# Splitting weights and building rotation tables in the first stage, keeping them in DRAM, and loading them per layer

## What is computed

```
for i in range(6):
    x = attn_layer(shift_tokens(x), Wqkv[i], q_scale[i], k_scale[i], Wo[i]) + x
    x = ffn_layer(shift_tokens(x), ln_g[i], ln_b[i], W1[i], b1[i], W2[i], b2[i]) + x

attn_layer:  q, k, v = split(x @ Wqkv)             # 128 -> 3 x 1024, 16 heads of 64
             q, k = l2norm(q) * q_scale, l2norm(k) * k_scale
             q, k = rotary(q), rotary(k)            # by position, with a scale
             out = local_attention(q, k, v) @ Wo    # windows of 32, each looks at itself and the one before
ffn_layer:   hg = (layernorm(x) * ln_g + ln_b) @ W1 + b1   # 128 -> 2 x 341
             a, gate = split(hg);  out = (a * gelu(gate)) @ W2 + b2
```

## Time and profile before

| | |
|---|---|
| runs of the kernel before | 3352.69, 3348.1, 3351.99 us; median 3351.99 |
| profiled execution | 3352.12 us, its span 3350.4 us |
| PE busy | 3196.8 us (95%) |
| POOL busy | 2967.1 us (89%) |
| DVE busy | 2747.9 us (82%) |
| ACT busy | 2740.7 us (82%) |
| TensorE clock over the span | 0.984 of full |
| DMA queue of the transfers | 226.85 MB, 25.3% of 16 engines |
| first stage / second stage | up to about 409 us / the rest |

### The profile page before, as it was taken

The page is one execution under the profiler, slowest core; times in us unless marked ns, Lnnn a source line. Parts: engine busy times, 40 slices in busy tenths (PEclk is TensorE's granted clock), DMA queues, the critical chain, the costliest instruction groups (busy, mean ns, idle before and its releaser), DMA issues.

```text
span 3350.4 us, 158044 instructions
## 1 busy us (share of the span) xinstructions
PE 3196.8 (95%) x64569; PEld 2754.7 (82%) x64570; DVE 2747.9 (82%) x5172; ACT 2740.7 (82%) x4528; POOL 2967.1 (89%) x3534
## 2 busy tenths in 40 slices
PE   7999669999999999999999999999999999999997
PEld 5676458888888888888888888888888888888886
DVE  7777577888888888888888888888888888888886
ACT  4677557888888888888888888888888888888885
POOL 5677578999999999999999999999999999989995
PEclk9999889999999999999999999999999999999998
DMA  2000013222223222223222233222232222332222
GB/s 62 5 8 8 16 39 90 76 75 72 66 72 99 75 74 68 67 75 102 75 70 68 70 96 81 70 68 75 69 102 74 68 72 63 82 91 73 75 66 74
DMA packets 162047, 228.51 MB, mean 68 GB/s; under 512 B 42392, under 2 KB 60768, under 8 KB 161760
## 3 DMA queue, kind: packets, MB, share of 16 engines
q1 hardware_dynamic: 161888, 226.85, 25.3%
HBM read 21.00 MB, written 4.19 MB: 8 GB/s over the span
## 4 chain that ended last, share of the span: by engine, by line
PE 65%; POOL 12%; issue 7%; ACT 2%; DVE 2%; POOLq 0%; SPq 0%; DMA 0%; DVEq 0%; ACTq 0%
PE ring L1418 9%; PE ring L1377 8%; PE ring L1427 8%; PE proj L1368 7%; PE score L1396 6%; PE proj L1370 6%; PE proj L1369 6%; POOL by_cos L1253 4%; PE ring L1403 4%; PE ring L1480 3%; PE ring L1471 2%; POOL weightsb L1264 2%; POOL by_cos L1259 2%; PE ring L1473 2%; PE ring L1472 2%
## 5 line engine op out<-in xcount | busy, mean ns | idle before, releaser
L1253 POOL TENSOR_TENSOR by_cos<-by_cos,by_sin 128x1024 f32<-128x1024 f32 x384 | 916.1, 2386 | 19.5 <-DVE by_sin L1654 19.4
L1259 POOL TENSOR_TENSOR by_cos<-by_cos,norms 128x1024 f32<-128x1024 f32 x384 | 731.6, 1905 | 20.1
L1652 DVE TENSOR_TENSOR by_cos<-proj,turns 128x512 f32<-128x512 f32 x768 | 521.7, 679 | 189.0 <-PE ring L1377 117.3
L1368 PE MATMUL proj<-qkv_hi,xs_hib 128*128 128x512 f32 x1152 | 535.5, 465 | 36.1 <-ACT vb L1515 16.0
L1654 DVE TENSOR_TENSOR by_sin<-proj,turns 128x512 f32<-128x512 f32 x768 | 522.5, 680 | 0.0
L1536 ACT ACTIVATE squares<-proj 128x512 f32<-128x512 f32 x768 | 444.1, 592 | 26.7 <-PE proj L1370 13.8
L1658 DVE TENSOR_REDUCE sumsb<-squares 128x16 f32<-128x1024 f32 x384 | 464.0, 1208 | 0.0
L1370 PE MATMUL proj<-qkv_hi,xs_lob 128*128 128x512 f32 x1152 | 459.5, 399 | 0.0
L1369 PE MATMUL proj<-qkv_lo,xs_hib 128*128 128x512 f32 x1152 | 459.2, 399 | 0.2 <-issue 0.2
L1377 PE MATMUL ring<-ident,by_cos 128*128 128x128 f32 x3072 | 413.2, 278 | 1.2 <-issue 1.2
L1418 PEld LDWEIGHTS ring<-pTb,v_win 64*64 64x64 f32 x24576 | 382.7, 136 | 36.7 <-issue 26.6
(11 more groups left out here) (188 smaller groups left out, 7349.7 us busy)
## 6 DMA issues: line engine op xcount, KB each, us to landing
v_win<-vb SPq DMA_DIRECT2D x1152, 128.0 KB, 2.3
v_win<-vb SPq DMA_DIRECT2D x768, 64.0 KB, 2.0
in_qkv<-L_ffn_Wqkv SPq DMA_DIRECT2D x12, 768.0 KB
wo<-L_ffn_Wo SPq DMA_DIRECT2D x12, 256.0 KB, 3.8
x_tok<-L_attn_x SPq DMA_DIRECT2D x8, 256.0 KB, 4.4
residual<-x_tok SPq DMA_DIRECT2D x8, 256.0 KB, 2.0
in_w<-L_ffn_W SPq DMA_DIRECT2D x12, 170.5 KB
in_qkv<-residual SPq DMA_DIRECT2D x1, 1536.0 KB, 6.7
```

The costliest lines, as they stand in the source:

```text
L1253: nc.gpsimd.tensor_tensor(both, both, by_sin[:, j, :], ALU.add).then_inc(e[f"{w_}_added"].sem, 1)
L1259: nc.gpsimd.tensor_tensor(heads, heads, inverse, ALU.mult).then_inc(e[f"{w_}_ready"].sem, 1)
L1368: nc.tensor.matmul(out, xs_hi[:, tile], qkv_hi[:, cols], start=True, stop=False)
L1652: nc.vector.tensor_tensor(of_heads(by_cos[:, t % 2, j, cols]), heads, table(0), ALU.mult)
```

## The change

- 48 pieces (36 of `Wqkv`, 128x512, and 12 of `W1`, 128x341) are split in the first stage. SP loads each four steps ahead, ScalarE copies the high part at the end of steps 1, 5, 7, 9, 13, 15 of each batch, VectorE subtracts one step later, SP stores the low part to DRAM. The `Wqkv` pieces of layer 0 come last and stay in SBUF.
- In batches 0 to 5 GpSimd makes the four tables of one layer at steps 5, 6, 12, 13, after `causal` and before `negated_maxima`. They are stored to DRAM, except those of layer 0, which stay.
- Per layer SP loads `Wqkv` and `W1` as before, and now their low parts too. ScalarE copies the high and then the low part of each `Wqkv` piece at the places of the `hi_*` pieces, and `NF` copies `w1_hi` and `w1_lo`. VectorE's `lo_*` and GpSimd's `turn_*` and `NL` are gone.
- The tables arrive by DMA (`Tq`, `Tk`), and `b1`, `ln_g`, `ln_b`, `W2`, `b2` (`FC`, `F2`, eleven transfers) go by DMA straight into the tiles in use.
- The second stage's prologue has no copies, subtracts or tables. The clears of `kT` and `v` are cut to the parts that are read before they are written, and the other padding is cleared by GpSimd there and no longer by VectorE at the start.

```diff
+SPLIT_AT = [MQA_H * b + h for b in range(B) for h in (1, 5, 7, 9, 13, 15)]
+TURN_AT = (5, 6, 12, 13)
...
             for n, b, h in steps():
                 if 0 <= n < HEADS:
                     causal(n)
+                if batch_of(b) and b < DEPTH and h in TURN_AT:
+                    rotation_table(DEPTH - 1 - b, TURN_AT.index(h))
                 if h % PER_GROUP == 1 and 0 <= (n + AHEAD) // PER_GROUP < B * GROUPS:
                     negated_maxima((n + AHEAD) // PER_GROUP)
...
+            def split_high(i):
+                kind, layer, k, slot, turn, cols = piece_of(i)
+                act.wait_ge(split_moved[slot], 32 * turn + 16)
+                copy(ready["hi"][:, cols], ready["in"][:, cols]).then_inc(split_hi, 1)
...
                     if 0 <= n < HEADS:
                         exps(n, k)
+                if n in SPLIT_AT:
+                    split_high(SPLIT_AT.index(n))
...
+            def split_low(i):
+                cols = piece_of(i)[-1]
+                dve.wait_ge(split_hi, i + 1)
+                nc.vector.tensor_tensor(ready["lo"][:, cols], ready["in"][:, cols], ready["hi"][:, cols].bitcast(F32),
+                                        ALU.subtract).then_inc(split_lo, 1)
...
+                if n - 1 in SPLIT_AT:
+                    split_low(SPLIT_AT.index(n - 1))
...
 NEXT_WEIGHTS = {
     "Act": {(-2, "aQq:3"): "hi_q0", (-2, "MK:1"): "hi_k0", (-2, "bQk:3"): "hi_k1", (-2, "GEL"): "hi_q1",
           (-1, "EV:1"): "hi_v0", (-1, "EK:0"): "hi_v1"},
-    "DVE": {(-2, "XM"): "lo_q0", (-2, "AM"): "lo_q1", (-2, "WX:-1"): "lo_k1", (-2, "XN"): "lo_v0 lo_k0",
-          (-1, "aCk:2"): "lo_v1"},
-    "Pool": {(-2, "Aq:3"): "turn_0", (-1, "Mk:0"): "turn_1", (-1, "Mq:1"): "turn_2", (-1, "Mk:1"): "turn_3"},
+    "SP": {(-2, "VM:1"): "Tq", (-1, "VM:0"): "Tk", (2, "VM:0"): "FC F2"},
 }
...
-            nc.gpsimd.memset(kT[:, :, :], 0.0)
+            nc.gpsimd.memset(kT[:, :, HS - WINDOW:HS], 0.0)
             nc.gpsimd.memset(sums[:, :, :, :, 1], L2_EPS2)
-            for n in range(TILES):
-                nc.gpsimd.memset(v[:, n, :, :, :], 1.0)
+            nc.gpsimd.memset(w2[:, FC - 1, :], 0.0)
+            for x in (in_w1, in_w1_lo):
+                nc.gpsimd.memset(x[:, :, FF:FC * P], 0.0)
+            nc.gpsimd.memset(col[:, :], 0.0)
...
                 elif kind[:3] == "hi_":
                     x = kind[3:]
-                    act.wait_ge(loaded, all_loaded(new))
-                    if when[1] >= 0:
-                        event, tile = f"{x[0]}_proj", PER * STEPS - 1 - PER * p
-                        wait_tile(act, event, tile, when, 1 + int(x[1]))
+                    act.wait_ge(qkv_loaded, new * 64)
+                    wait_tile(act, f"{x[0]}_proj", PER * STEPS - 1 - PER * p, when, 1 + int(x[1]))
                     cols = columns_of(x)
-                    copy(qkv_hi[:, cols], in_qkv[:, cols]).then_inc(p_hi[x], 1)
+                    copy(qkv_hi[:, cols], in_qkv[:, cols]).then_inc(p_qkv[x], 1)
+                    copy(qkv_lo[:, cols], in_lo[:, cols]).then_inc(p_qkv[x], 1)
                 elif kind == "NF":
-                    act.wait_ge(loaded, all_loaded(new))
-                    wait_half(act, "gated", when, 0)
-                    wait_half(act, "xn_lo", when, 0)
-                    copy(col[:, :], in_col[:, :]).then_inc(p_col, 1)
+                    act.wait_ge(w1_loaded, new * 48 + 48)
                     wait_half(act, "up_full", when, 0)
                     copy(w1_hi[:, :, :], in_w1[:, :, :]).then_inc(p_w1_hi, 1)
-                    wait_half(act, "y_full", when, 0)
-                    copy(w2[:, :, :], in_w2[:, :, :]).then_inc(p_w2, 1)
+                    copy(w1_lo[:, :, :], in_w1_lo[:, :, :]).then_inc(p_w1_lo, 1)
```

More of the change, by code:

```diff
@@ L118, in fills, with piece_of, mqa_stage @@
     return (3, FILLS * m), (2, FILLS * m + 1), (1, FILLS * m + 2)
-def mqa_stage(nc, c, semaphore, weights, x_in, credits, arrived, residual, first_layer):
+def piece_of(i):
+    kind, layer, k = SPLITS[i]
+    slot, turn = i % len(PIECES), i // len(PIECES)
+    n = INNER // 2 if kind == "qkv" else FF
+    return kind, layer, k, slot, turn, slice(slot * (INNER // 2), slot * (INNER // 2) + n)
+def mqa_stage(nc, c, semaphore, weights, x_in, credits, ready, kept, of_layer, tables_in, residual):
     with ExitStack() as ctx:
@@ new lines, in load_split, with store_split @@
+            def load_split(i):
+                kind, layer, k, slot, turn, cols = piece_of(i)
+                at_least(sp, split_moved[slot], 32 * turn)
+                if kind == "qkv":
+                    in_ = of_layer["Wqkv"][layer, :, k * (INNER // 2):(k + 1) * (INNER // 2)]
+                else:
+                    in_ = of_layer["W1"][layer, :, k * FF:(k + 1) * FF]
+                sp.dma_start(ready["in"][:, cols], in_).then_inc(split_moved[slot], 16)
+            def store_split(i):
+                kind, layer, k, slot, turn, cols = piece_of(i)
+                sp.wait_ge(split_lo, i + 1)
+                if kind == "qkv":
+                    out = kept["qkv"][layer, :, k * (INNER // 2):(k + 1) * (INNER // 2)]
+                else:
+                    out = kept["w1"][layer, :, k, :]
+                sp.dma_start(out, ready["lo"][:, cols].bitcast(F32)).then_inc(split_moved[slot], 16)
@@ L899, in steps_of @@
     if at == -LEAD:
-        steps += [((piece,), None, "", 0) for piece in " ".join(NEXT_WEIGHTS.get(engine, {}).values()).split()]
+        steps += [((piece,), None, "", 0) for piece in ("FC", "F2") if engine == "SP"]
     if at == -LEAD and engine == "SP":
@@ L911, in steps_of @@
             steps.append((("NO",), 0, "", tile // (PER * STEPS)))
-        if engine == "Pool" and name == "FP" and at is not None and at % STEPS == LAG and end is None:
-            steps.append((("NL",), 0, "", at // STEPS))
         steps.append(((name,), t, token, 0 if tile is None else tile // (PER * STEPS)))
@@ L1196, in new_layer @@
                 sp.sem_inc(sp_ready, 1)
-                load_layer(sp, arrived, w, layer + 1)
+                for k in range(2):
+                    half = slice(k * QKV // 2, (k + 1) * QKV // 2)
+                    sp.dma_start(in_qkv[:, half], w["Wqkv"][one, :, half].rearrange("a k n -> (a k) n")).then_inc(qkv_loaded, 16)
+                    sp.dma_start(in_lo[:, half], kept["qkv"][one, :, half].rearrange("a k n -> (a k) n")).then_inc(qkv_loaded, 16)
+                sp.wait_ge(p_w1_hi, layer + 1)
```

238 lines of the change are left out of this document (136 added, 102 removed).

## The result

The changed kernel takes 3330.28 us (median of 5; 3329.26 to 3337.39) against 3351.99 (median of 5): a ratio of 0.9944, with a 95% interval of 0.9930 to 0.9958. It is 0.56% faster. The prediction was 3344 with a range of 3326 to 3364: the sign and the range held, but the gain was 22 us in place of the forecast 8, nearly three times as much.

A forecast was written before the change was run, and what follows sets the result against it. TensorE was taken to bound the second stage, so only layer changes, prologue and first stage could move. -6.6 (prologue) - 18.6 (A) - 0.5 (B) + 17 (stage one) = -8.7 on 3352.1 gave 3344 us, range 3326 to 3364.

The forecast's parts named there:

- part A: Cycles renewing Wqkv pieces and tables at a layer change: excess 4.1 in place of 7.8 us, -18.6 us over five.
- The rule on the shared interface: VectorE with two SBUF inputs and GpSimd reading SBUF take turns, the later blocking for the whole other; speaks against the change.
- rival 4: Stage one: each of 48 subtracts costs its full 0.67 us beside GpSimd; 3363 us, 3373 with mutual waits; chance 0.14.
- Part B: Later cycle renewing FFN weights: `vb` wait some 0.2 us longer, `w_lo` gone; about -0.1 x 5, -0.5 us.
- Prologue: Start of stage two: narrow clears, no copies or subtracts, first projection earlier by 6.6 us (bounds -5.5 and -8).
- Stage one: First stage, which receives the 48 pieces and the tables: +17 us (bounds +5 to +37).
- The sum for the tables: Stage one, GpSimd tables: +0.6 us at h=5, +0.4 at h=13, others in idle time; 4.7 us over six batches.
- rival 1: Stage one hides the subtracts in VectorE's idle time; only about 5 us reach TensorE, 3332 us; chance 0.19.
- transitions nearly free: Layer changes: ScalarE's copies also find cover, A falls to about 1 us; 3329, with rival 1 3320; chance 0.08.
- Rival 3: Layer changes: ScalarE takes it back, doubled copies return the idle elsewhere, A gains at most 1 us each; 3357; chance 0.13.

The follow-up runs named there:

- the subtracts alone: Changed kernel with the six low parts of a layer change made again by VectorE's subtracts, without ScalarE's low copies; tables still by transfer: 3341.7 us.
- the products alone: Changed kernel plus four unused GpSimd products of 128x256 at a layer change, where the rotation tables were made before: 3344.4 us.
- both: Changed kernel with VectorE's subtracts back in place of ScalarE's low copies, and four GpSimd products at the old tables' places: 3350.7 us.

## Why the prediction was right, point by point

- **The layer change, part A.** An excess of 4.1 us in place of 7.8 was worked out, 3.8 measured: -19.9 us over five changes for -18.6. The steps behind it hold one by one: the mean 4.1 us late was worked out and 3.7 measured, the transpose of `weights` behind TensorE's own order, `weights` ready 1.0 us before it, the clock at 1.00. What the prediction left undivided, two causes of GpSimd's delay, the runs divide: the subtracts alone bring back 2.27 of the 2.90 us and the lower clock at two changes of five, the products alone nothing, both 2.72 us and the lower clock at all five.
- **The rule on the shared interface.** Each kernel with subtracts beside GpSimd in stage two shows an operation of 0.25 us that takes 2.6 and ends with the subtracts. In stage one a key spreading of 1.56 us takes up to 2.1 with a subtract beside it. The Trainium skill, SBUF — State Buffer, section "Who interferes with whom", says that a VectorE instruction with two inputs in SBUF contends with a GpSimd one that reads SBUF. The traces agree with that, but not with a block for the length of one other instruction, as the prediction put it: the GpSimd operation began before the subtracts and was held over three of them. The price in stage one was 0.2 us per subtract and not the 0.67 of rival 4.
- **Part B.** -0.1 us was forecast for each layer, -0.6 measured (1.9 to 1.3 over the cycles of that place). The wait for `vb` is as worked out (1.33 against 1.3). What failed is the reading of `w_lo`: the 0.27 us that I took for the lateness of `f_rstd` is only GpSimd's idle time between the two instructions. In the kernel before:

```profile
1005.50 0.16 DVE L1727 TENSOR_SCALAR f_varb<-ring 128x2 f32<-128x2 f32 x1 [0.74 <-PE ring L1455]
...
1005.64 1.85 POOL L1316 TENSOR_TENSOR w_lo<-in_w,w_hi 128x768 fp32r<-128x768 f32 x1
```

  The variance was ready at 1005.66, and `f_rstd` started at 1007.76, 2.1 us later; in the changed kernel it starts 0.1 us behind the variance (1005.63 + 0.16, 1005.87). So 2.0 us of lateness went, and not 0.3. How they become 0.6 us of TensorE's time was not tested by itself.
- **Prologue.** -6.6 forecast, -7.1 measured.
- **Stage one.** +17 forecast, +15.0 measured. Of the terms, the tables hold (0.87 us per batch) and ScalarE's copies cost nothing. The subtracts cost 1.2 us in a full batch and not 2.0: idle time took in more than I had counted, towards rival 1; at which steps was not read. The sum for the tables doesn't follow from its own terms: 0.6 and 0.4 in each of six batches are 6.0 us, and 4.7 was put down. Batches 1 to 6 sum to +10.2 us; the other 5 lie in the first batch and the last (+3.6 and +1.8, less 0.6 at the start), which differ by 1.5 and 3.2 between two traces of the kernel before.
- **What was not in the sum.** -4.6 us between the first projection and the first `f_rstd`, and -3.1 us at the end. Both places vary by several us among kernels with the same work there, and the end by 3.5 between two traces of one kernel. The two make more than half of the 13.7 us between forecast and median (3344 less 3330.3); the rest is mostly the layers (3.2), stage one (2.0) and the prologue (0.5). The sum itself gives 3343.4, which was written as 3344. So the mechanism of the layer change was right, and the number fell inside the range, but the forecast of 8 us for the whole was far from the 22 measured, mainly because the sum had no term for these two places.

The rivals: transitions nearly free (1 us) and ScalarE taking it back (7) are both excluded by 3.8, and subtracts at their full price by 0.2 us each. Rival 3 needed the wait for `weights` to return, and it didn't. The first, stage one hidden (5 us), is excluded by the trace although its total, 3332, is nearer to the result than my own: that is luck.

## What to carry to other kernels

Work that delays an engine off the critical path is dear when the bound engine then idles in one long piece and its clock falls; spread over three short waits, 3.0 us of idle came with 3.8 us of excess, while the kernel before paid 7.8 in the mean for 2.9 us in one piece and the short ones ahead of it. An idle time that the profile shows just ahead of an instruction is not how late that instruction is: the lateness is counted from when its input was ready (2.1 us at `f_rstd`, where the idle time said 0.27). Before an operation is put into "idle" steps, ask what stands behind it in that engine's order: a share of idle time isn't slack where the next instruction is awaited. Where a copy only renews a tile that has a moment of disuse, let the transfer write the tile itself, and look at which engine waits for its landing.

## What was unexpected of the hardware

Waits of TensorE of the same length, 2.23 to 2.27 us in the same place of the cycle, left the granted clock at 1.00 at three layer changes and at 0.83 over the next 10 us at two, which cost 1.2 us each; waits of 2.7 us and more lowered it each time. So the 6.9 and 8.2 us of one kernel at equal work are a matter of the clock. By the profile, a GpSimd operation of 0.25 us was held for 2.57 us over three subtracts of VectorE, although it had begun first. And two traces of one kernel differed by 5 us at the clears, 3.2 of them in the last batch of stage one, where TensorE has little to do and its clock falls at different moments.
